# One decoder layer pair on one NeuronCore: the same three instruction streams merged in another order

## What is computed

```python
x = ln(x + attn_taylor(x))        # a: 16 heads, rope, weights 1 + s + s*s/2
x = ln(x + attn(x, ctx, mask))    # b: 16 heads, softmax, projections with biases
x = ln(x + experts(x))            # c: 8 experts 256->512->256, each computed for all tokens
x = ln(x + delta_rule(x))         # d: short convs, chunkwise delta rule, 31-tap filters, gate
x = ln(x + attn(x, ctx))          # e: 16 heads, softmax, no projections
x = ln(x + fp4_ffn(x))            # f: gate/up/down with values rounded to FP4 blocks of 16
```

## Time and profile before

| what | value |
|---|---|
| median of 3 runs | 4067.72 us (4062.06 to 4068.14) |
| the profiled execution | 4060.48 us, its span 4058.7 us |
| PE busy | 3306.0 us, 81% of the span |
| DVE busy | 2622.4 us, 65% |
| ACT busy | 1637.3 us, 40% |
| granted TensorE clock, mean | 0.932 |

### The profile page before, as it was taken

The page is one execution under the profiler, slowest core; times in us unless marked ns, Lnnn a source line. Parts: engine busy times, 40 slices in busy tenths (PEclk is TensorE's granted clock), DMA queues, the critical chain, the costliest instruction groups (busy, mean ns, idle before and its releaser), DMA issues.

```text
span 4058.7 us, 64443 instructions
## 1 busy us (share of the span) xinstructions
PE 3306.0 (81%) x22532; PEld 2516.1 (62%) x22532; DVE 2622.4 (65%) x5927; ACT 1637.3 (40%) x3066; POOL 341.9 (8%) x696
## 2 busy tenths in 40 slices
PE   1678988889797988889798888979798888978664
PEld 0456766767575766667576676757566666756452
DVE  4324667585776767576676758577676757666653
ACT  1423453544435354444435354443535444342311
POOL 1000101010100101010100101010010101010100
PEclk9788999999999999999999999999999999999766
DMA  2011211121111112111121111111111211111000
GB/s 71 21 58 47 64 37 53 35 57 42 45 48 38 53 35 64 35 51 42 38 55 38 53 35 56 42 42 47 43 53 35 60 38 51 42 33 54 9 6 3
DMA packets 185756, 175.65 MB, mean 43 GB/s; under 512 B 59208, under 2 KB 147936, under 8 KB 185440
## 3 DMA queue, kind: packets, MB, share of 16 engines
q1 hardware_dynamic: 185440, 171.27, 14.6%
HBM read 156.55 MB, written 14.68 MB: 42 GB/s over the span
## 4 chain that ended last, share of the span: by engine, by line
PE 38%; issue 26%; DVE 25%; ACT 6%; POOL 2%; DMA 1%; PEld 0%; SPq 0%; PEldq 0%; DVEq 0%; ACTq 0%; POOLq 0%
PE bank L703 13%; DVE region L1796 4%; PE bank L938 4%; PE bank L791 3%; ACT pt_f L1200 3%; DVE nm_f L1577 2%; PE bank L737 2%; PE bank L771 2%; PE bank L1020 1%; PE bank L784 1%; PE bank L1099 1%; PE bank L1031 1%; POOL rn L672 1%; ACT qT_f L1221 1%; PE bank L1040 1%
## 5 line engine op out<-in xcount | busy, mean ns | idle before, releaser
L1200 ACT ACTIVATE pt_f<-bank 128x512 f32<-128x512 f32 x768 | 416.2, 594 | 281.5 <-PE bank L771 280.9
L938 PE MATMUL bank<-c_w,c_hb 128*128 128x256 f32 x2048 | 511.1, 389 | 10.0 <-PEq L1173 6.6
L703 PE MATMUL bank<-xTc,c_w 128*128 128x256 f32 x2048 | 488.9, 388 | 16.4 <-DVE yc L1729 15.7
L1796 DVE SCALAR_TENSOR_TENSOR region<-vpad,cols,region 128x256 f32<-128x256 f32 x1024 | 450.5, 481 | 15.4
L938 PEld LDWEIGHTS bank<-c_w,c_hb 128*128 128x128 f32 x2048 | 378.2, 193 | 98.1 <-issue 26.0
L703 PEld LDWEIGHTS bank<-xTc,c_w 128*128 128x128 f32 x2048 | 383.9, 193 | 79.5 <-DVE yc L1729 21.3
L737 PE MATMUL bank<-identb,split_f 128*102 128x128 bf16 (+1 forms) x4096 | 296.6, 241 | 151.1 <-DVE split_f L1562 109.6
L1299 ACT ACTIVATE c_hb<-bank,cols 128x256 f32<-128x256 f32 x512 | 215.0, 471 | 484.5 <-PE bank L703 484.5
L737 PEld LDWEIGHTS bank<-identb,split_f 128*102 128x102 bf16 (+1 forms) x4096 | 284.2, 144 | 181.7 <-issue 124.8
L1577 DVE TENSOR_REDUCE nm_f<-bank 128x2 f32<-128x512 f32 x512 | 315.9, 685 | 122.5 <-PE bank L758 119.2
L771 PE MATMUL bank<-qT_f,kT_f 102*128 102x256 bf16 (+1 forms) x1536 | 276.1, 282 | 116.0 <-ACT pt_f L1200 91.6
(11 more groups left out here) (310 smaller groups left out, 5442.9 us busy)
## 6 DMA issues: line engine op xcount, KB each, us to landing
c_w<-in_c_w SPq DMA_DIRECT2D x256, 512.0 KB, 3.8
gram_scratch<-region SPq DMA_DIRECT2D x32, 256.0 KB, 2.1
x<-in_x SPq DMA_DIRECT2D x16, 256.0 KB, 4.2
x<-in_ctx SPq DMA_DIRECT2D x16, 256.0 KB, 4.4
ctxb<-in_ctx SPq DMA_DIRECT2D x16, 256.0 KB, 3.6
out_dram<-x SPq DMA_DIRECT2D x16, 256.0 KB, 2.3
region<-gram_scratch SPq DMA_DIRECT2D x128, 8.0 KB
inverse_scratch<-region SPq DMA_DIRECT2D x32, 64.0 KB
```

Of the source, the lines that this page charges most:

```text
L703: mm = pe.matmul(out_ap, l, r, start=(i == 0), stop=(i == len(pairs) - 1))
L938: mm = pe.matmul(PS[use][:, t * D:(t + 1) * D], c_hb[:, k, t * P:(t + 1) * P], c_w2[:, e % W_SLOTS, k, :], start=(k == 0), stop=(k == HC - 1))
L1200: act.activation(dst, PS[use].rearrange("p (c s) -> p c s", c=c), func, **kw).then_inc(*PS.drained(use))
L1796: ins = dve.scalar_tensor_tensor(dst[:, c, :], x, w_[:, c, k:k + 1], dst[:, c, :], ALU.mult, ALU.add)
```

## The change

Only the list `BODY` is another one. Every segment is still there once, each stream keeps its order, and no instruction is added, removed or altered. A comparison of the two lists shows, from the start of a pass: `c_in` and `c_gate` come after `e_turnk` and `e_max0`; `c_down0a` moves from before `e_score0` to after `e_score1`, `d_conv` between those two; `c_down0b` and `e_score2` come after `d_silu`; `e_score3` comes after `d_token` and `d_norm`; `e_out` directly follows `e_weigh3`; `c_up1b` comes between `a_norm` and `a_proj`, `c_down1a` after `a_proj`; `d_gram` moves behind `a_rope`, `d_grams` behind `a_part2`; `d_place` moves behind `f_round1`. After `f_round1`, `d_one4` comes behind `a_weigh1` and expert 4 with `d_two4` behind `a_weigh3`, where both stood between `f_round1` and `a_weigh3`; `c_down7b` comes before `b_score1`, and `c_apply` before `b_res`.

```diff
--- before.py
+++ after.py
@@ -98,16 +98,16 @@
 
 
 BODY = """
-e_in e_part1 e_part2 d_in c_in e_turnq e_turnk c_gate e_max0 d_proj e_max1 c_comb e_max2 c_up0a e_max3 c_up0b e_shift
-e_again c_down0a e_score0 e_score1 e_weigh0 e_score2 d_conv d_silu e_weigh1 c_down0b e_score3 d_token e_weigh2
-e_weigh3 c_up1a d_norm e_out c_up1b c_down1a d_chan a_norm e_res d_gram a_proj e_apply f_in a_rope d_blocks d_grams
-f_up0 a_part1 f_up1 a_part2 c_down1b a_turnq c_up2a c_up2b c_down2a f_round0 d_fir0 d_place c_down2b a_turnk c_up3a
-c_up3b c_down3a f_round1 d_fir1 c_down3b c_up4a c_up4b d_fir2 f_down d_fir3 f_res d_one4 f_apply d_fir4 a_score0
-c_down4a a_score1 d_two4 a_weigh0 a_score2 a_weigh1 c_down4b a_score3 a_weigh2 a_weigh3 d_twb4 d_one5 a_out d_fir5
-b_in d_two5 b_ctx a_res c_up5a a_apply c_up5b b_x d_twb5 d_one6 d_fir6 d_two6 b_proj b_part1 d_sums c_down5a d_scan0
-b_part2 c_down5b d_scan1 c_up6a b_turnq b_turnk d_scan2 b_max0 d_scan3 b_max1 d_turn d_gate d_gated b_max2 c_up6b
-b_max3 b_shift d_logit c_down6a b_again d_weight c_down6b b_score0 d_mix b_score1 c_up7a c_up7b b_weigh0 b_score2
-b_weigh1 c_down7a b_score3 b_weigh2 b_weigh3 d_ms d_out b_out d_res c_down7b d_apply c_res b_res c_apply b_apply
+e_in e_part1 e_part2 d_in e_turnq e_turnk c_in e_max0 c_gate e_max1 d_proj e_max2 c_comb e_max3 c_up0a e_shift c_up0b
+e_again e_score0 d_conv e_score1 c_down0a d_silu e_weigh0 c_down0b e_score2 e_weigh1 d_token d_norm e_score3 e_weigh2
+e_weigh3 e_out c_up1a d_chan a_norm c_up1b e_res a_proj e_apply c_down1a f_in a_rope d_gram d_blocks f_up0 a_part1
+f_up1 a_part2 d_grams c_down1b a_turnq c_up2a c_up2b c_down2a f_round0 d_fir0 c_down2b a_turnk c_up3a c_up3b c_down3a
+f_round1 d_place d_fir1 d_fir2 c_down3b f_down f_res f_apply a_score0 a_score1 a_weigh0 a_score2 a_weigh1 d_fir3
+d_one4 a_score3 a_weigh2 a_weigh3 d_fir4 c_up4a a_out b_in c_up4b b_ctx a_res c_down4a a_apply d_two4 c_down4b c_up5a
+d_twb4 b_x d_one5 c_up5b d_fir5 b_proj d_two5 b_part1 c_down5a d_twb5 b_part2 c_down5b d_one6 d_fir6 d_two6 d_sums
+c_up6a d_scan0 b_turnq b_turnk c_up6b d_scan1 b_max0 c_down6a d_scan2 b_max1 c_down6b b_max2 d_scan3 c_up7a b_max3
+d_turn d_gate d_gated c_up7b b_shift b_again d_logit c_down7a d_weight d_mix b_score0 c_down7b b_score1 b_weigh0 c_res
+b_score2 b_weigh1 d_ms b_score3 b_weigh2 b_weigh3 d_out b_out d_res c_apply d_apply b_res b_apply
 """.split()
 assert [n for n in BODY if n[0] in "efab"] == ONE
 assert [n for n in BODY if n[0] == "d"] == TWO and [n for n in BODY if n[0] == "c"] == THREE
```

## The result

The changed kernel is slower, by 0.44%. 22 runs of it have a median of 4086.32 us (4054.90 to 4118.95), 22 runs of the kernel before, taken beside them, 4067.47 us (4062.06 to 4076.79); the ratio is 1.0044, with a 95% interval of [1.0027, 1.0061]. The forecast was 4013, and 4062 was the end of its range. The single times of the changed kernel spread over 64 us, those of the kernel before over 15. One of the changed kernel's 22 runs, 4118.95, lies more than 1.5% above its fastest and is left out of the ratio; without it the spread is 51 us. The profiled run took 4091.95 us, its span is 4090.2 us, 31.5 us over that of before.

The account below looks back on a forecast made before the run. PE, busy 81% of the span, was taken as the main bound. Stretch gains of 1.4 and 2.5 us made 3.9 a pass, 55 us in all: 4005.5 from the profiled 4060.5, or 4013 against the runs' median; range 3985 to 4062.

Parts of the forecast that it names:

- xTf's wait: PE's wait at L703 ahead of a_proj: from 2.98 us to near 0.5 us.
- hf's at L816: New PE wait at e_out for the evacuation of the last sums: 0.75 us.
- hf's at L712: New PE wait for DVE ahead of a_norm's transposes: 1 to 1.5 us.
- qT_f's: New PE wait at L771, where e_score0 waits for ACT's copies: 1 us.
- about half: Share of PE's 32 idle us in a pass taken to be fractions of a microsecond between records.
- The stretches: Turn of the loop to e_again: 0; e_again to f_round0: minus 1.4 us; f_round1 to the pass's end: minus 2.5.
- the clock's fall moves from b_proj to c_up6a, at the same price: Behind d_one6 and d_two6: the fall moves, still costing some 1.5 us, so counted as 0.
- one fall that goes (1.6 us): At a_proj: without the long idle time the clock should stay up, shortening PE's a_proj by 1.6 us.
- The prediction's own signs of being wrong: A pass of 231 us or more, mean clock below 0.96, or DVE busy through the second stretch while PE waits.
- R3: Slower: new clock falls from e_score0 to e_out and in scans with b maxima; three a pass, 4080 us; chance 0.10.
- R1: The clock falls at a_norm as well, taking back 1.6 us a pass: 4034 us; chance 0.22, with like cases.
- R2: DVE keeps the first stretch and holds PE in the second: gain 0 to 0.6 us a pass, 4060 to 4068; chance 0.12.

Follow-up runs that it names:

- first_back: The changed kernel with everything ahead of f_up0 put back in the order of before; 4022.36 us, ratio to the kernel before 0.9884.
- gram_late: first_back with d_gram moved behind a_rope; 4057.21 us, ratio to the kernel before 0.9974.
- turn_fill: first_back with 14 overwritten products added behind d_in, in the idle time at the turn of the loop; 4052.11 us, ratio to the kernel before 0.9954.
- first_back_again: first_back, unchanged, for ten more runs; 4035.80 us, ratio to the kernel before 0.9926.
- fill_before: The kernel before with two down products done twice on PE, ahead of f_round0 and f_round1; 4086.23 us, ratio to the kernel before 1.0037.
- second_back: The changed kernel with everything behind f_round1 in the order of before; 4084.85 us, ratio to the kernel before 1.0031.
- after_d2: The changed kernel with two overwritten products of 0.22 us added ahead of c_up7a in each pass; 4081.69 us, ratio to the kernel before 1.0041.
- fill_rounds: The changed kernel with two down products done twice on PE, ahead of f_round0 and f_round1; 4074.87 us, ratio to the kernel before 0.9999.
- before_d1: The kernel before with one overwritten product of 0.22 us added ahead of c_up7a in each pass; 4091.14 us, ratio to the kernel before 1.0057.
- grams_early: The changed kernel with d_grams moved back directly behind d_blocks; 4091.53 us, ratio to the kernel before 1.0046.

## Why the prediction was wrong

**The waits: right.** In the pass with 17.1 us low, as many as before though in part in other places, the length is 228.5 us against 228.2 in the sum. xTf's wait is 0.4 (forecast 0.5), hf's at L816 0.7 (0.75), hf's at L712 0.9 (1 to 1.5), qT_f's 0.9 to 1.1 (1). a_proj is at full clock in 3.70 us (3.6), the waits of the earlier trace rows are gone or down to 0.3, and DVE is busy 162 us for 161. One reading of the page was wrong without changing the sum: "about half" of PE's 32 idle us were called fractions between records. The waits of that pass add up to 30 us; left out were 3.7 for x (L712, three times) and 2.2 for the split ahead of e_again and b_again (L737 for L1587), which is 0.3 in the changed kernel.

**The stretches: right in sign, the first one split otherwise.** From e_turnq to f_round0 it was 87.5 us (1490.7, one pass ahead of 1722.76, to 1578.15); in the short pass it is 879.76 - 794.53 = 85.2: minus 2.3. f_round0 to f_round1 was to stay at 11.8 and is 893.21 - 879.76 = 13.45: plus 1.7, the fall. Together minus 0.6, where minus 1.4 was forecast. From f_round1 to b_res it was 1709.11 - 1589.94 = 119.2 and is 1008.67 - 893.21 = 115.5, minus 3.7; from there to the next e_turnq 14.2 for 13.65, plus 0.6: minus 3.1, where minus 2.5 was forecast. The step "the clock's fall moves from b_proj to c_up6a, at the same price" did not hold in this pass, where that fall is missing altogether; in the pass of 235.6 us c_up6a takes 3.78 us at half clock, as forecast, and this stretch takes 120.7. So the 228.5 that lies so near the sum is in part luck: more was gained in both stretches than forecast (2.3 and 3.1), and a fall at f_round0 that was not in the sum took 1.7 back, while the one at c_up6a that was in it is missing. Nor does the first stretch's gain show in the other orders: first_back, which goes without it, has passes of 228.7.

**What failed: the clock as a constant.** The sum priced one fall that goes (1.6 us) and one that moves (0), and put new ones at nothing, holding all others at what the earlier trace rows show. That is the step that failed. The runs put a mean of 29.9 us low in a pass in its place, 12.2 more than before. By 0.44 that is 5.4 us, against 3.6 gained: plus 1.8 a pass, which is 233.9 - 232.1; the line was drawn through these same passes, so this shares out the difference and does not test it. In the profiled runs the thirteen full passes carry 20.7 of the 31.5 us, pass 16 and what follows 16, and the start gives 5 back. The prediction's own signs of being wrong came: nine of thirteen passes have 231 us or more, at a mean clock of 0.91 to 0.95.

**The rivals.** R3, with a chance of 0.10, is the mechanism that came, and near its price (4080 against 4086): the new falls cost more than the gain. Its count was right, 39 falls at places without one before, which is three in each of thirteen passes, but its places were mostly not: e_score has a fall in 2 passes, c_comb or c_up0a in 5, and the one at c_up6a and the scans, in 10, is the one that had been forecast to move. It did not name the two roundings, 19 falls, nor the scores of a, 13, from which c_up4 and c_down4a were taken away. So its number was met in part by luck. R1 did not come: the clock stood at 1.00 at a_norm in the window shown, and no full pass has a fall between 21 and 71 us. The reason given against R1, that "the 1.8 us waits before both f_rounds show no fall", was a true reading, and wrong as a bound: it was taken as if a wait of that length were safe. At f_round1 the same 1.8 us have a fall in 7 of 13 passes of the changed kernel, while at f_round0 2.1 us stand without one in gram_late. The length of the wait alone does not decide. R2 did not come.

Of transposes and the clock, the runs show 64 of them in 3.77 us after 0.80 us of idle time in turn_fill, at full clock, and in 5.57 to 6.34 after 6 to 9 us. The Trainium skill, "TensorE: Matmul & The Clock Gate", Part 4, says that they do not count as busy work in the same way. No run here separates that from the waits around them. The Trainium skill, on the same page in Part 1, says that the gate does not start its count with the kernel, so that the number of cold matmuls at the start of one kernel varies from run to run, and that for modelling this warm-up is below 1% of a typical kernel's time. The first would fit the two groups of first_back, but no run shows it to be their cause. The second speaks of one warm-up; here falls recur in each pass, the two groups lie 45 us apart, 1.1%, and every version compared lies within 2.0% of the others.

**Open.** Shown is that low time makes most of the difference between equal passes, that a fall goes when the wait ahead of it is filled, and that on the kernel before 0.22 us of work a pass brings new ones. What exactly decides whether the clock falls at a place in a given pass is not shown; where one fall comes, the pass gets longer and the next places are met differently, which would explain alternating passes, but is only argued. Nor is it shown why first_back settles on one of two lengths. The same lengths come back in kernels with other orders, waits and work: 232.0 to 232.3 us in all of the first twelve full passes of before and first_back_again, in ten of fill_before, nine of second_back and eight of after_d2, and 228.6 to 228.8 in all of first_back and three of gram_late. So the length of a pass is not simply the sum of its work and waits, and its agreement with such a sum is weaker evidence for the terms than it looks. The best version found, first_back, is by its two ratios 0.7 and 1.2% faster than the kernel before, and each of its 14 runs is below the median of the kernel before taken beside it.

## What to carry to other kernels

Where PE is the bound and its clock falls in each pass, put the falls into the sum as a term of its own with a range, and count as candidates all places where PE waits about as long as it does somewhere else with a fall, or works in short pieces; that a place has none now, or that an equal wait has none elsewhere, is no proof. After a change read the time at half clock pass by pass, over all passes, before looking for a stall: equal waits with unequal pass lengths point to the clock. An order written from instruction times of one trace carries that trace's clock in it, so time several orders, with many runs each, and expect that edits do not add up.

## What was not expected

- One program without any input that differs ran in 4018 to 4024 or in 4061 to 4066 us in nine of ten runs (first_back_again), and its full passes but the last are alike in each of the two that were profiled.
- Work added to idle time made one kernel faster (fill_rounds, 0.45%) and the same work made the other slower (fill_before, 0.37%).
- 3.5 us of products cost 22 us (before_d1).
- Taking a fall away where it stood did not mean less low time on the whole (grams_early, turn_fill).
- One us at half clock costs 0.31 to 0.50 us of the pass, much as if PE bounded nearly everywhere the clock falls.
